# A macaron layer on one core: where the first rows of the closing feed-forward layer are normalised

## The reference

```python
x = x + 0.5 * ffn(layernorm(x))        # 512 x 512 weight, dequantised, plus LoRA and bias
x = x + attn(layernorm(x))             # x -> h = x + mamba2(rmsnorm(x)); h + mlp(rmsnorm(h))
x = x + 0.5 * ffn(layernorm(x))        # the closing layer, the same weights as the first
```

## Time and profile before

| | us |
|---|---|
| median of 3 runs | 834.28 |
| lowest and highest | 832.6, 834.89 |
| the profiled execution | 835.37 |
| its span in the profile | 833.6 |

### The profile page before, as it was taken

The page is one execution under the profiler, slowest core; times in us unless marked ns, Lnnn a source line. Parts: engine busy times, 40 slices in busy tenths (PEclk is TensorE's granted clock), DMA queues, the critical chain, the costliest instruction groups (busy, mean ns, idle before and its releaser), DMA issues.

```text
span 833.6 us, 10783 instructions
## 1 busy us (share of the span) xinstructions
PE 771.6 (93%) x3560; PEld 358.9 (43%) x3560; DVE 648.7 (78%) x1247; ACT 432.3 (52%) x845; POOL 350.2 (42%) x389
## 2 busy tenths in 40 slices
PE   7987799999899699998889899999999999996898
PEld 3433354454455344443334344444444444442343
DVE  4799778978868975757798797797888878756884
ACT  2685566766655555535444545555555546442431
POOL 4523344563533255657742224225124233223654
PEclk9999999999999999999998999999999999999899
DMA  8622332231210012100060262554553643432555
GB/s 301 149 50 47 71 60 51 52 89 27 51 26 14 13 26 87 27 13 13 1 152 13 39 152 52 101 137 77 120 105 68 152 77 71 82 64 39 132 147 127
DMA packets 93559, 64.01 MB, mean 77 GB/s; under 512 B 67472, under 2 KB 74640, under 8 KB 93504
## 3 DMA queue, kind: packets, MB, share of 16 engines
q1 hardware_dynamic: 80448, 40.15, 18.5%
q0 software_dynamic: 12672, 23.07, 15.6%
q10 hardware_dynamic: 384, 0.10, 0.1%
HBM read 20.32 MB, written 4.19 MB: 29 GB/s over the span
## 4 chain that ended last, share of the span: by engine, by line
PE 50%; DVE 5%; ACT 2%; DMA 2%; POOL 1%; issue 1%; SPq 0%; ACTq 0%; DVEq 0%; POOLq 0%
PE PS L1835 47%; PE PS L1963 2%; DMA raw_d<-down_t 1%; PE PS L1953 0%; DVE raw L1432 0%; ACT raw_gu L971 0%; DVE xs L1773 0%; DMA raw_gu<-n_p 0%; DVE xs L1696 0%; PE PS L1928 0%; DVE mk L1373 0%; DVE raw L1433 0%; DVE n L1429 0%; ACT w_in L1019 0%; DVE pre L1679 0%
## 5 line engine op out<-in xcount | busy, mean ns | idle before, releaser
L669 POOL DMA_DIRECT2D xs<-x x59 | 51.8, 883 | 154.6 <-ACT x L1057 152.3
L1835 PE MATMUL PS<-h,w_in 128*128 128x512 f16 x480 | 112.0, 387 | 2.5 <-DMA h<-hn_p 1.4
L1835 PE MATMUL PS<-h,x_t 128*128 128x512 f16 x408 | 95.6, 384 | 3.4 <-DVEq L1404 3.4
L1835 PEld LDWEIGHTS PS<-h,w_in 128*128 128x128 f16 x480 | 47.5, 100 | 69.7 <-issue 19.2
L1835 PE MATMUL PS<-n_T,stage 128*128 128x512 f16 x288 | 71.5, 379 | 4.1 <-DVE xs L1773 2.2
L478 POOL TENSOR_TENSOR r<-mv,mhalf 128x1 f32<-128x1 f32 (+1 forms) x32 | 27.2, 849 | 87.2 <-DVE mv L1179 68.2
L1835 PEld LDWEIGHTS PS<-h,x_t 128*128 128x128 f16 x408 | 39.9, 99 | 53.4 <-issue 8.5
L1057 ACT ACTIVATE x<-PS,d_d 128x512 f32<-128x512 f32 x59 | 40.1, 679 | 42.3 <-PE PS L1835 36.2
L669 POOL DMA_DIRECT2D xs<-n x29 | 25.9, 894 | 72.4 <-ACT n L1057 71.0
L1835 PE MATMUL PS<-w_ffn,raw_gu 128*128 128x512 f16 x192 | 45.4, 393 | 7.5 <-DMA raw_gu<-n_p 7.5
L1028 ACT ACTIVATE xds<-tm,dgh 128x512 f32<-128x512 f32 x24 | 17.3, 722 | 62.2 <-DVE tm L1760 62.2
(11 more groups left out here) (311 smaller groups left out, 1825.2 us busy)
## 6 DMA issues: line engine op xcount, KB each, us to landing
xs<-x POOLq DMA_DIRECT2D x59, 256.0 KB, 3.3
xs<-n POOLq DMA_DIRECT2D x29, 256.0 KB, 3.2
x_t<-x_in SPq DMA_DIRECT2D x16, 256.0 KB, 3.0
out<-x_t SPq DMA_DIRECT2D x16, 256.0 KB, 2.3
raw_gu<-gate_t SPq DMA_DIRECT2D x7, 512.0 KB, 4.6
raw_gu<-up_t SPq DMA_DIRECT2D x7, 512.0 KB, 5.6
raw_d<-down_t SPq DMA_DIRECT2D x7, 512.0 KB, 6.0
raw<-w_in_t SPq DMA_DIRECT2D x4, 642.0 KB, 9.6
```

What stands on the lines that cost most here:

```text
L669: po.dma_start(chunk_of(xs, c), d_tmps[d % 3], accum_op=ALU.add).then_inc(s_acc[d % 3], 16)
L1835: ins = pe.matmul(out_, lhs(a, b, k), rhs(a, b, k), start=first and n == 0, stop=last and n == len(todo) - 1)
```

## The change

Three things are moved; no instruction is added or dropped.

- On GpSimd, `c_norm` of rows 0 to 2 stands between the adding DMAs of unit 23: row 0 after the second, row 1 after the third, row 2 after the fourth. Row 3 follows.
- On ScalarE, `c_hi` of rows 0 and 1 stands before and after the last eviction of unit 23, row 2 after its last tanh. Row 3 comes after `hi_s(23, 1)`. The four float32 buffers are given out in another order, so that n0 belongs to row 3, and row 3 has the wait for the adding DMA.
- On VectorE, each `tail` of unit 23 is one place earlier: `tail(0)` ahead of the add of IP7, `tail(1)` ahead of the adds of IP5, `tail(2)` ahead of that of IP3, `tail(3)` ahead of that of IP4. `c_lo(0)` stands behind `tail(2)`, `c_lo(1)` behind `tail(3)`. After the unit comes `c_lo(2)`, then `tail(4)`, `tail(5)`, `c_lo(3)`.

```diff
-        c_n = [n0[:, :], hn[:, :], h2n[:, :], n1[:, :]]
+        c_n = [hn[:, :], h2n[:, :], n1[:, :], n0[:, :]]
...
-            for m in range(NU):
-                unit(m)
...
-            for c in range(NC):
-                c_norm(c, c % NC)
+            for m in range(NU - 1):
+                unit(m)
+            last_downs = downs_of(NU - 1)
+            x_add(last_downs[0])
+            x_add(last_downs[1])
+            c_norm(0, 0)
+            x_add(last_downs[2])
+            c_norm(1, 1)
+            x_add(last_downs[3])
+            c_norm(2, 2)
+            c_norm(3, 3)
...
                 weight_work(p, n, 1 if n == 2 else 2)
+                if m == NU - 1:
+                    c_hi(0, 0)
                 if len(ds) > 2:
                     evict(ds[3])
                 if n == 2:
                     weight_work(p, n, 2)
+                if m == NU - 1:
+                    c_hi(1, 1)
                 tanh_s(m, 1)
...
+                if m == NU - 1:
+                    c_hi(2, 2)
 
             def c_hi(c, k):
-                if c == 0:
+                if c == NC - 1:
                     ac.wait_ge(*added(max(d for d in range(N_D) if d % 3 == 2)))
...
-            for c in range(NCH):
+            for m in range(NU):
+                unit(m)
+            hi_s(NU - 1, 0)
+            hi_s(NU - 1, 1)
+            for c in range(NC - 1, NCH):
                 c_hi(c, c % NC)
...
+                if m == NU - 1:
+                    tail(0)
                 ve.wait_ge(e_gu, 2 * NS + base + 4)
                 ve.wait_ge(e_add, base + 2)
                 ve.tensor_tensor(u3[k], u2, p_bank(m, IP7), ALU.add).then_inc(e_add, 1)
...
                 if m == NU - 1:
-                    tail(0)
+                    tail(1)
                 ve.wait_ge(e_gu, 2 * NS + base + 5)
...
                 if m == NU - 1:
-                    tail(1)
+                    tail(2)
+                    c_lo(0, 0)
                 ve.wait_ge(e_gu, 2 * NS + base + 6)
...
                 if m == NU - 1:
-                    tail(2)
+                    tail(3)
+                    c_lo(1, 1)
                 ve.wait_ge(e_gu, 2 * NS + base + 7)
                 ve.tensor_tensor(u3[k], u3[k], p_bank(m, IP4), ALU.subtract).then_inc(e_add, 1)
-                if m == NU - 1:
-                    tail(3)
...
-            c_lo(0, 0)
-            c_lo(1, 1)
+            c_lo(2, 2)
             tail(4)
-            c_lo(2, 2)
             tail(5)
             c_lo(3, 3)
```

## The result

| | runs | median us | lowest to highest |
|---|---|---|---|
| before | 4 | 833.96 | 832.6 to 834.89 |
| changed | 4 | 821.66 | 819.86 to 823.42 |

The ratio is 0.9858, with a 95% interval of 0.9839 to 0.9876: 11.8 us faster, where 12.2 were forecast. The profiled execution of the changed kernel took 821.48 us, its span 819.7 (forecast: about 821.4).

What follows compares the result with a forecast made beforehand. TensorE bounds the kernel, standing still near its end: 12.66 us to be had, less 0.5 for bias adds, gives 12.2, so 822.1 us from the median 834.28 (chance 0.74); range 820.4 to 825.0.

Steps and rivals of the forecast that it cites:

- The ceiling: TensorE from the unit's third down product to `down_tail(6)`: twelve groups need 15.54 us, took 28.20, so 12.66 to be had.
- The low clock's 2.2: Part of the 12.66 us: `c_f(0)` behind the hole ran at low clock, 4.76 us for two groups instead of 2.59.
- The tails: VectorE's `tail(0)` to `tail(3)` one place earlier end TensorE's waits ahead of `down_tail(1)` to `(3)`: 0.3, 0.9, 1.6 us saved.
- The powers: GpSimd's `c_norm` between the adding DMAs costs 1.28 us each; no adding DMA waits for anything new.
- `c_hi` and `c_lo`: ScalarE's `c_hi` takes 1.5 us; VectorE's `c_lo(0)` at 758.6, transpose landing 762.0, 1.0 us ahead of `c_f(0)`: no hole.
- the prediction's own list: Signs of being wrong: over 1 us wait ahead of `c_f(0)` or `c_f(3)`, clock under 1.00, TensorE waits behind `c_f(4)`.
- The bias adds: GpSimd's bias adds beside the unit's end and `c_lo(3)` lengthen VectorE's work: 0.5 us lost, between nothing and 1.2.
- The transposes: SP's row transposes ahead of the `c_f` products were each counted as landing 2.73 us after issue.
- "It costs nothing": Other order of buffers on ScalarE: only row 0 no longer needs n0, an adding DMA's source; cost nothing.
- Rival A: Transposes share DMA engines with the last adding DMA, so first products wait: gain 8.5 to 10.5 us, about 825; chance 0.14.
- Rival B: Any first product 2.4 us late lowers the clock again: 2.4 + 1.9 lost, gain 8.4, 825.9; chance 0.07.

Runs made afterwards that it cites:

- the run with the homes turned: Changed kernel with the float16 buffers of the four rows turned by one, row 0 in raw_d, row 3 in h2n_p: ratio to before 0.9857, stretch 27.85 us.

## Why the prediction was right

**The ceiling** of 12.66 us, counted in groups of six matmuls, was exact: its part up to `down_tail(6)` was gained in full. The low clock's 2.2 measured 2.15, alone. The split that the expectations made of it, ahead of those runs, between the tails (4.0 against 3.83) and the rest (8.0 against 8.20) held.

**The tails** came where the schedule put them: `tail(2)`'s sum was in time with its 0.3 to spare, and no tail made TensorE wait.

**The powers** between the adding DMAs took 0.92 to 1.30 each and held no DMA; moving them behind, and `c_hi(0)` with them, costs 1.7.

**`c_hi` and `c_lo`**: `c_lo(0)` stood at 756.35, 8.48 behind the third down product, forecast 8.5 (758.6 against 750.11).

**The wait that is left** is where the sum was off: 1.05 ahead of `c_f(3)` where 0.5 stood, so 11.6 in the stretch and not 12.2. By the prediction's own list, a wait of over 1 us there was a sign of being wrong, and it came, if barely. Two terms made it.

*The bias adds* had the 0.5 for themselves, and that was about right: 1.08 + 0.35 - 0.9 = 0.53, or 0.65 by the run with the homes turned, where the landing was 2.7. It was right partly by luck, as a choice between ends whose parts were both off: the first meeting cost 1.08 (0.27 or 1.27 counted), the second 0.35 (0.27 or 0.8). The 0.95 at 771.46 misled: that `c_lo` came in when the bias add was nearly over, so 0.27 was the rest of a wait and not the price of one. The silu product, issued early in the bias add, waited 1.08. In the Trainium skill, SBUF — State Buffer, Who interferes with whom, this is full exclusion; the 1.72 and 1.76 side by side agree with it.

*The transposes* were counted at 2.73 throughout, though the trace of before had longer ones out of raw_d. Row 3's, out of raw_d, took 3.15: 0.4 of the wait, for which the sum had no term. Row 0's took 3.5 and kept 0.2 of its 1.0 us to spare.

**"It costs nothing"**, said of the new order of the buffers, holds, but the step saw only half of what that order does. It looked only at when row 0 is ready. With the old order the last adding DMA starts with the first transpose, and the stretch is 0.95 us longer: the new order gains that. The expectation of the run, that the order costs and gains nothing, was wrong. Rival A named that collision, but as chance and not as what this edit avoids.

**Rival B** took from one wait in one profile that 2.4 us bring the low clock. That happened in eleven of fourteen profiles. Its 1.9 for the low clock is 1.7 from group to group (466.52 to 470.81 in the profile before, against 2.59). Its condition never came: the longest wait in the stretch was 1.05 here, and 2.00 with the old order.

**What the time alone tells** is less than this. The interval of the ratio is 10.3 to 13.4 us and holds 11.6, the forecast 12.2 and the ceiling 12.66 alike. The profiled span came out 1.7 us under its forecast although the stretch gained 0.6 less than the sum: the last unit began 2.24 us earlier, which nobody forecast, and which lies within the scatter of that start. That part is luck.

## What to carry to other kernels

Count the bottleneck engine's work in equal groups over the stretch that a change touches, and subtract: the difference is the ceiling, and here it held to a tenth of a microsecond. Then lay out the other engines' orders in that time and look at the margins of a microsecond or less; there, take each transfer at the landing time of its own source buffer, count what else starts with it, and for each VectorE operation with two SBUF inputs what GpSimd does beside it, at the full length of that operation. An edit that only delays a transfer nobody waits for can still cost something, if it then starts beside one that is waited for.

## What the runs showed of the hardware

- A transposing DMA and an adding DMA from GpSimd, issued within 0.3 us of each other, landed after 4.5 to 5.7 and 4.3 to 5.4 us instead of 2.7 and 3.3; with the transpose 1 us ahead they landed after 2.7 and 3.3.
- An adding DMA with no transpose in flight took 4.8 and 5.0 us in two runs, where a 16 KB packet of the instruction queue came 2.8 us after its issue. That the packet is the cause was not tried.
- Transposes of the same size out of raw_d landed after 3.0 to 3.2 us in most cases and out of the other three buffers mostly after 2.7, whichever row they carried. Single ones took longer, up to 3.7 in the steady rounds of the changed kernel, and 4.6 for its last. Why the source matters was not tried.
- A GpSimd bias add issued 0.1 us into a VectorE product with two inputs in SBUF took 1.72 us instead of 1.27, and the VectorE product behind it 1.76 instead of 0.68.
- Thirty matmuls of zeros in a hole of 7.6 us, whose last 1.0 us stayed empty, kept the granted clock at 1.00.
- After one and the same wait of 2.4 us the granted clock had fallen in eleven of fourteen profiles and not in three.
